# One fused front stage reordered: relayout of batches 0 to 2 ahead of the last unit's chain, head norm of the last unit pair on VectorE and ScalarE, last batch first

## The reference, cut to what matters

```python
qkv = _layernorm(x) @ w_qkv                      # 16 heads of width 8, each split in halves q1,q2 / k1,k2
a = softmax(q1 k1' / sqrt(8)) - lam * softmax(q2 k2' / sqrt(8))
out = a @ v
rms = jnp.sqrt(jnp.mean(out * out, axis=-1, keepdims=True) + 1e-6)     # the head norm, over 8 values
out_n = out / rms * norm_w[None, :, None, :] * (1.0 - LAMBDA_INIT)
out_cat = out_n.reshape(b, H * s, HD)
x = x + out_cat.transpose(0, 2, 1).reshape(b, s, e) @ wo
# cross attention with 32 context rows per batch
h = _layernorm(x)
logits = h ctx' * 128 ** -0.5 + mask * -1e9
x = x + softmax(logits) @ ctx
```

## Time and profile before

| | us |
|---|---|
| median of 3 runs | 1115.52 (1113.68 to 1121.27) |
| profiled execution, its own time | 1116.36 |
| its span | 1114.6 |
| TensorE busy in the span | 950.8 |
| VectorE busy | 778.4 |
| ScalarE busy | 621.1 |
| GpSimd busy | 466.8 |

### The profile page before, as it was taken

The page is one execution under the profiler, slowest core; times in us unless marked ns, Lnnn a source line. Parts: engine busy times, 40 slices in busy tenths (PEclk is TensorE's granted clock), DMA queues, the critical chain, the costliest instruction groups (busy, mean ns, idle before and its releaser), DMA issues. The chain is left out here.

```text
span 1114.6 us, 21183 instructions
## 1 busy us (share of the span) xinstructions
PE 950.8 (85%) x6168; PEld 489.8 (44%) x6168; DVE 778.4 (70%) x1612; ACT 621.1 (56%) x1537; POOL 466.8 (42%) x708
## 2 busy tenths in 40 slices
PE   3479999999999985699879999999999986854493
PEld 1112223323323233366555555555555553653393
DVE  7798999999999955466646666566566657855252
ACT  4638888888888861222156665665665542421162
POOL 4222544544544554000034454554544436763452
PEclk9759999999999996699989999999999997975797
DMA  3010000000000000000010000000000000007354
GB/s 83 7 30 1 1 2 2 1 0 0 0 0 0 0 1 1 0 15 22 18 34 9 15 9 8 10 11 7 7 14 8 1 1 1 1 4 167 100 174 132
DMA packets 45227, 24.96 MB, mean 22 GB/s; under 512 B 11976, under 2 KB 43520, under 8 KB 45168
## 3 DMA queue, kind: packets, MB, share of 16 engines
q1 hardware_dynamic: 43920, 21.66, 7.5%
q0 software_dynamic: 1248, 2.57, 0.7%
HBM read 19.08 MB, written 5.15 MB: 22 GB/s over the span
## 5 line engine op out<-in xcount | busy, mean ns | idle before, releaser
L640 DVE TENSOR_REDUCE a_nmax<-a_rows 128x2 f32<-128x1024 f32 x256 | 299.2, 1218 | 14.9 <-PE a_rows L487 11.6
L754 ACT ACTIVATE a_probs<-a_turned 128x512 f32<-128x512 f32 x512 | 269.9, 604 | 50.4 <-PE a_turned L509 48.8
L1175 POOL TENSOR_TENSOR a_prob<-a_prob,a_rinv 128x256 f32<-128x256 f32 (+3 forms) x128 | 159.7, 1253 | 173.0 <-DVE a_rinv L1365 172.8
L1358 DVE TENSOR_REDUCE a_nmax<-a_score 128x2 f32<-128x256 f32 (+3 forms) x128 | 105.6, 825 | 125.4 <-PE a_score L1214 120.9
L1312 ACT ACTIVATE a_prob<-a_score,a_nmax 128x128 f32<-128x128 f32 (+3 forms) x256 | 132.5, 523 | 82.5 <-DVE a_nmax L1358 82.2
L509 PE MATMUL a_turned<-a_q,a_qk 32*128 32x512 bf16 x512 | 138.2, 393 | 6.1 <-ACT a_probs L754 4.5
L472 PE MATMUL a_acc<-a_probs,a_vg 128*32 128x512 f32 x1024 | 140.3, 621 | 0.8 <-ACT a_probs L754 0.7
L487 PE MATMUL a_rows<-a_qk 32*128 32x512 bf16 x512 | 111.9, 402 | 13.2 <-DVE a_nmax L640 5.9
L1211 PE MATMUL a_score<-a_k_s,a_q_s 64*128 64x384 f32 (+3 forms) x512 | 103.7, 481 | 2.2 <-ACT a_prob L1312 1.3
L509 PEld LDWEIGHTS a_turned<-a_q,a_qk 32*128 32x128 bf16 x512 | 35.2, 91 | 154.0 <-ACT a_probs L754 128.6
L1371 DVE COPY a_pt<-a_turn 128x128 f32<-128x128 f32 (+3 forms) x224 | 92.2, 447 | 1.4 <-PE a_turn L1225 1.4
(11 more groups left out here) (302 smaller groups left out, 1593.0 us busy)
## 6 DMA issues: line engine op xcount, KB each, us to landing
m_w<-L_ffn_w SPq DMA_DIRECT2D x23, 256.0 KB
a_wq<-L_attn_Wq SPq DMA_DIRECT2D x16, 128.0 KB, 2.0
m_w_all<-L_ffn_w SPq DMA_DIRECT2D x4, 512.0 KB, 11.2
xs_sorted<-m_blank SPq DMA_DIRECT2D x1, 1495.0 KB, 11.7
m_xs<-xs_sorted SPq DMA_DIRECT2D x5, 260.0 KB, 5.5
g_X<-x SPq DMA_DIRECT2D x4, 256.0 KB, 3.7
g_m_wgu<-L_ffn_gate_up_proj SPq DMA_DIRECT2D x8, 128.0 KB, 2.1
a_wk<-L_attn_Wk SPq DMA_DIRECT2D x32, 32.0 KB, 1.8
```

What stands on the lines that cost most here:

```text
L640: dve.tensor_reduce(nmax[i % 2][:, p // 2, (p % 2) * 2:(p % 2) * 2 + 2], rows[n % 2][:, :, :], AX_X, ALU.max, negate=True).then_inc(row_ou ...
L754: act.activation(probs[:, (tb % 2) * 4 + j, :], turned[n % 3][:, :], ACT.Exp, scale=float(HD0) ** -0.5).then_inc(turn_out, 1)
L1175: pool.tensor_tensor(pr, pr, spread(rinv[:, t % RING, :], 2, width), ALU.mult).then_inc(scl, 1)
L1358: dve.tensor_reduce(nmax[:, t % RING, :], score[t % 2][:, :, 0:width], AX_X, ALU.max, negate=True).then_inc(mx, 1)
```

## The change

1. GpSimd: the relayout copies of batches 0, 1 and 2 move from the end of body 31 to just before unit 31's shift; that of batch 3 moves behind the layernorm roots of batches 1 and 2, and these move behind the head norm of units 28 and 29.
2. The division and head norm of the last pair leave GpSimd. VectorE does them in `last_pair`, with a `Sqrt` on ScalarE between a sum and a reciprocal.
3. TensorE: the projections move from steps 9, 11, 13 of body 31 to steps 11 and 14 of body 31 and 1 of body 32; of the turns of rows only two stay inside body 32 (steps 9 and 13), the third and all logits come behind the last `out_turn`. Batch 3's projection comes ahead of `logits_of(2)` and of all of the cross attention.
4. VectorE: the last pair comes ahead of `vector_copy(2)` and all `soften`; batch 3's residual and norm come ahead of the cross attention's additions; the second norm of batches 1 to 3 comes last. ScalarE follows that order.

```diff
@@ y_of, TensorE
-                pe.wait_ge(comb, QUADS // 2 * (b + 1))
+                if b < B - 1:
+                    pe.wait_ge(comb, QUADS // 2 * (b + 1))
+                else:
+                    pe.wait_ge(comb, QUADS // 2 * B - 1)
+                    pe.wait_ge(last_done, 1)
@@ body, TensorE
-                    if i == N - 1 and k in (9, 11, 13):
-                        y_of((k - 9) // 2)
-                    if i == N and k in (6, 9, 12):
-                        rows_turn((k - 6) // 3)
-                    if i == N and k in (10, 14):
-                        logits_of((k - 10) // 4)
+                    if (i, k) in ((N - 1, 11), (N - 1, 14), (N, 1)):
+                        y_of(((N - 1, 11), (N - 1, 14), (N, 1)).index((i, k)))
+                    if (i, k) in ((N, 9), (N, 13)):
+                        rows_turn((k - 9) // 4)
@@ before_last, VectorE
-                soften(0)
-                ln.vector_copy(dve, 2)
-                soften(1)
+
+            def last_pair():
+
+                link = Chain(dve, lastc)
+                dve.wait_ge(rl, N // 2)
+                half2 = rsum[:, :, :].rearrange("p (n a) u -> p n a u", a=2)[:, :, 1, :]
+                link(dve.tensor_tensor(half2, half2, neglam[:, 0:1].unsqueeze(2).broadcast_to([P, 2 * SB, 2]), ALU.mult))
+                dve.wait_ge(comb, N // 2 - 1)
+                o = o_tok[:, :, :].rearrange("p n (u w) -> p n u w", w=HW)[:, :, :, 0:HD0]
+                link(dve.tensor_tensor(o_n[:, :, :, :], o, spread(rsum[:, :, :], 3, HD0), ALU.mult))
+                o = o_n[:, :, :, :].rearrange("p (t h a) u d -> p a h t (u d)", h=2, a=2)
+                link(dve.tensor_tensor(both[:, :, :, :, :].rearrange("p h t u d -> p h t (u d)"), o[:, 0], o[:, 1], ALU.add))
+                pairs = both[:, :, :, :, :].rearrange("p h t u d -> p (h t u) d")
+                link(dve.tensor_tensor(sq[:, :, :], pairs, pairs, ALU.mult))
+                link(dve.reduce_sum(ms[:, :], sq[:, :, :], AX_X))
+                dve.tensor_scalar(ms[:, :], ms[:, :], HD0 * 1e-6, None, ALU.add).then_inc(last_ms, 1)
+                dve.wait_ge(last_rt, 1)
+                link(dve.reciprocal(rms[:, :], rms[:, :]))
+                link(dve.tensor_tensor(pairs, pairs, spread(rms[:, :], 2, HD0), ALU.mult))
+                for u in range(2):
+                    n = N - 2 + u
+                    last = dve.tensor_tensor(cat[:, n // QUADS, :, n % QUADS, :].rearrange("p d (h t) -> p h t d", t=SB),
+                                             both[:, :, :, u, :], spread(nw[:, n, :, :], 2, SB), ALU.mult)
+                last.then_inc(last_done, 1)
...
@@ ScalarE, behind the bodies
-            for b in range(3):
-                cross_exp(b)
-            for b in range(3):
-                cross_copy(b)
-            ln2.scalar(act, (0, 1, 2))
+            act.wait_ge(last_ms, 1)
+            act.activation(rms[:, :], ms[:, :], ACT.Sqrt).then_inc(last_rt, 1)
+            cross_exp(0)
+            cross_exp(1)
+            cross_copy(0)
+            cross_exp(2)
+            cross_copy(1)
             ln.scalar(act, (3,))
+            cross_copy(2)
             cross_exp(3)
             cross_copy(3)
-            ln2.scalar(act, (3,))
+            ln2.scalar(act)
@@ body, GpSimd
                     pool.tensor_copy(qs[u][:, :, :], g.q_tok[:, i + SIX * r, :, :]).then_inc(cut, 1)
+                    if i == N - 1:
+                        for b in range(3):
+                            lay_out(b)
...
                 if i == N:
-                    ln.gpsimd(pool, (0, 1, 2))
-                if has_norm(i):
+                    ln.gpsimd(pool, (0,))
+                if has_norm(i) and i < N + 2:
...
+                if i == N:
+                    ln.gpsimd(pool, (1, 2))
+                    lay_out(3)
```

More of the change, by code:

```diff
@@ L615, in _ @@
             run(pe, body)
+            logits_of(0)
+            rows_turn(2)
+            logits_of(1)
+            y_of(3)
             logits_of(2)
[L617 to L621 removed]
+            cross_of(0)
+            cross_of(1)
             rows_turn(3)
             logits_of(3)
+            cross_of(2)
             cross_of(3)
[L625 removed]
+            for b in range(B):
+                rows_turn2(b)
         @block.vector
@@ L707, in before_last @@
                 ln.vector_copy(dve, 1)
-                soften(0)
-                ln.vector_copy(dve, 2)
-                soften(1)
-            run(dve, body)
+            def last_pair():
[20 more added lines that the diff above has]
+                last.then_inc(last_done, 1)
+            run(dve, body)
+            last_pair()
+            ln.vector_copy(dve, 2)
+            soften(0)
+            soften(1)
+            residual(3)
             soften(2)
             cross_sum(0)
+            ln.vector_norm(dve, (3,))
             cross_add(0)
```

34 lines of the change are left out of this document (12 added, 22 removed).

## The result

The kernel after took 1112.12 us in the median of 20 runs (1101.51 to 1114.69), the kernel before 1116.56 in 20 runs beside it (1113.28 to 1121.64). The ratio is 0.994, 95% interval 0.992 to 0.9959. The forecast was 1104.7 us with a range up to 1109.6: too fast by 7.4 us, and the time lies outside the range. The profiled execution took 1114.54 (span 1112.8, mean granted clock 0.901) against 1116.36 (1114.6, 0.916).

What follows compares the result with a forecast made beforehand. TensorE was taken as the limit until 421 us, no engine after. Front 6.5 plus tail 4.8 gave 11.3 us off: 1105.1 from the profiled execution, 1104.2 from the median, middle 1104.7 us, range 1101.5 to 1109.6.

Steps and rivals of the forecast that it cites:

- so what it gains the program gains: Whole stage between two barriers: its gain of 11.3 us was taken as the gain of the whole program.
- Front, 6.5 us: Body 31 to the last pair's reciprocal: reciprocal at 414.5 instead of 421.00, a gain of 6.5 us.
- the old stall: TensorE's 2.70 us wait for the first relayout copy; without it no clock fall was expected, gaining another 1.7 us.
- the new wait: TensorE ahead of batch 1's turn of rows, waiting for its norm behind GpSimd's head norm: loss of 1.3 us.
- The shift L850: Unit 31's shift on GpSimd: a start after 393.8 was to show the forecast wrong.
- Rival 2: Front's clock falls at TensorE's added wait, 407 to 413: value groups cost 1.6 us more in all, 1106.3; chance 0.10.
- Tail, 4.8 us: Reciprocal to the end of the last norm: 27.3 us against 32.15, a gain of 4.8.
- The third product: TensorE's cross attention in the tail: lands about 1.5 us after VectorE wants it, charged as a wait.
- Rival 1: Tail runs at full clock: the 1.5 us wait goes, last turn shortens, 1.9 us more gain, 1102.8; chance 0.13.
- rival 3: Tail only shifts because one order is wrong: its 4.8 us shrink to nothing, 1109.5; chance 0.12.
- Table loads: ScalarE's switches between Exp and Sqrt around the last pair: both loads covered, by 1.0 and 1.6 us, costing nothing.
- Rival 5: Slower: GpSimd's chain for units 28 and 29 at half speed, about 11.5 us lost, 1117; chance 0.05.

Runs made afterwards that it cites:

- the repeated pair: Kernel before and kernel after each measured again without an edit: 1117.55 us (ratio 1.0005) and 1111.3 us (ratio 0.9928).
- r4_before_shift2: Kernel before with 2 chained memsets on VectorE at the end of the causal attention: 1123.02 us, ratio 1.0039.
- root early twice: Two runs of the kernel after with GpSimd's root of batch 1 ahead of units 28 and 29's head norm: 1102.77 us (0.987) and 1109.26 us (0.9907).
- r3_old_tail: Kernel after with the orders behind the loop taken back to those of the kernel before: 1117.44 us, ratio 1.0003.
- r1_after_again: Kernel after measured once more without an edit: 1111.3 us, ratio 0.9928.
- r3_pool_norm: Kernel after with only the last pair's head norm taken back to GpSimd: 1114.26 us, ratio 0.9956.

## Why the prediction was wrong

**The step that failed** is one sentence of the first part: barriers stand on both sides of the stage, "so what it gains the program gains". Barriers keep the work of the stages apart; they do not keep the length of a stage. Of the 11.26 us that the stage gained, 9.46 were lost behind it in the profiled pair: the cross stage grew by 5.45 us, with no instruction changed, the front of the last mixture by 1.80, mixture 0 with the route logits by 1.41. In the repeated pair 8.36 of 11.63 were lost, 6.43 of them in the cross stage. Where they were lost the clock was low for longer. r4_before_shift2 shows that a run with 1.2 us of added wait has this long cross stage in the kernel before. How the losses come about is shown by the stretches above; why the clock falls when it does stays open. Of four profiles with the new front and nothing added (after twice, root early twice) three have the fall at 1.50 to 1.62 and one at 1.96, all with a long stage; the two of the kernel before have 1.80 and 1.94 and a short one. Why just these distances come up I can't show. I had a warning on the page: the kernel before had run between 1113.68 and 1121.27 with the same code, and the chance for an outcome of this kind was nowhere in my list of rivals.

**Front, 6.5 us: 5.97 in the profiled pair**, 421.00 to 415.03, and 415.03 also in r3_old_tail. The relayout took 1.52 (said: 1.45), the clock was 1.00 (the fall behind the old stall is gone, though no run shows its 1.7 us by itself), the new wait was 1.39 (1.3). The shift L850 began at 394.01, beyond the 393.8 named as a sign of being wrong, but not because of the copies: GpSimd was idle 0.49 ahead of it, waiting for VectorE's maxima, and the loop ran 0.3 us later in that execution.

**Rival 2, the clock falls at the new wait,** did not come in the first profile and came in the second (r1_after_again): 0.55 between 409 and 412, with the reciprocal 2.83 us later, where its price was 1.6. The front's gain was 5.63 in that pair (423.49 to 417.86), since the kernel before also had a longer low stretch.

**Tail, 4.8 us: 5.32** (32.15 against 26.83). The last pair took 3.5 (3.6), `Sqrt` began 0.04 after its input at 417.23, the last norm ended at 441.86 (441.8). VectorE is busy 23.73 of 26.83, and it waited nowhere over 2 us after 418. The third product, for which I had charged 1.5, made it wait 0.70, and the second, for which I had charged nothing, 1.01. Rival 1 (full clock) did not come, the mean was 0.70, and neither did rival 3 (a tail that only shifts). That the two parts add up to 11.29 against 11.3 is in part luck: the front gave 0.5 less than its sum and the tail 0.5 more.

**The size of the moved head norm.** In r3_pool_norm it alone is worth 4.3 us. It had no term of its own in the sum. The tail's terms charged VectorE 3.3 us for it and named GpSimd's old chain only as the reason why batch 3's projection began late.

**Table loads** cost nothing, as forecast. The Trainium skill (ScalarE: Activation LUTs, What ACT_TABLE_LOAD costs) has a drain of 1.38 us at each switch. By the page's figure and this trace's load, as an estimate, the root could not have begun before 414.99 + 1.38 + 1.28 = 417.65. It began at 417.27 and was waiting for VectorE, so the trace disagrees with that drain here.

**Rival 5**, a slow chain on GpSimd, did not come: the head norm of units 28 and 29 ended at 406.49.

## What to carry to other kernels

In this program, where TensorE is half idle for long stretches, changes of its clock made stages several us longer or shorter, and behind the saving these changes came at other places. For a kernel of this kind, compare stage lengths with the clock of each, and judge a change by many runs or at equal clock before taking a difference of 5 us as its own. Undo a change part by part before crediting its parts: here two parts that were each worth nothing gave 11 us together. And put a repeat of the unchanged kernel beside the first experiment; its spread would have set a wider range.

## What was not expected of the hardware

- The clock stayed low in a stretch in which TensorE is recorded as busy throughout: 12.00 of 12 us between 447 and 459 at 0.50 in the kernel after.

```profile
447.00:459.00 12.00, 12.00 (x40) 8.92 (x39) 3.78 (x12) 3.63 (x5) 0.00 (x0) 0.50 0.00 0
```

- A wait of 1.21 us at the end of the causal attention went with a next stage longer by over 5 us (91.76 against 84.02 to 86.56).
- 16 matmuls with 8 columns (32 records) took 6.83 us at 0.50 and 3.72 where the clock rose in them; a group of wide ones (128x512) took 1.94 and 1.06 us at the two levels.
- Two executions ran the same 63 us of work to within 0.03 us, and then the clock fell in the one and not in the other.
- The runs of the kernel after differ by 13 us (1101.51 to 1114.69) and follow the mean granted clock at 5 us per 0.01.
